# Split register loads, prompt masks from a table in DRAM, and a moved GpSimd addition in a four-layer fused kernel

## The reference

```python
def reference(x, ...):
    x = x + _L0_cond_ref(x, fside_Bx2_0, condB_angle)      # rotate/shift each image, bilinear gather
    x = x + _L1_cond_ref(x, itok_B_0_7, ...)               # FFN 512->2048->512, plus low rank parts by expert
    x = x + _L2_cond_ref(x, L2_cond_W1, L2_cond_b1, L2_cond_v, itok_B_0_2)
    x = x + _L3_cond_ref(x, itok_B_0_8, ...)               # adapter by language, then layer norm
    return x

def _L2_cond_ref(hidden, W1, b1, v, prompt_type_ids):
    scores = jnp.einsum('bsa,a->bs', jnp.tanh(jnp.einsum('bsd,da->bsa', hidden, W1) + b1), v)
    prefix_m, postfix_m, cloze_m = l <= j, l >= j, l != j
    mask = jnp.where(pt == 0, prefix_m[None], jnp.where(pt == 1, postfix_m[None], cloze_m[None]))
    p = jax.nn.softmax(jnp.where(mask, scores[:, None, :], NEG_INF), axis=-1)
    return jnp.einsum('bjl,bld->bjd', p, hidden) / cnt[..., None]

# end of _L3_cond_ref: x = hidden_states + adapted
    normed = (x - mean) * jax.lax.rsqrt(var + LN_EPS)
    return normed * gamma[language_ids][:, None, :] + beta[language_ids][:, None, :]
```

## Time and profile before

| | |
|---|---|
| median of 3 runs | 2572.32 us |
| profiled execution, own time | 2575.34 us |
| its span, first to last instruction | 2573.5 us |
| PE busy | 2274.3 us (88%) |
| DVE busy | 2052.4 us (80%) |
| POOL / ACT busy | 935.1 (36%) / 872.3 (34%) |
| mean granted TensorE clock | 0.928 of full |

### The profile page before, as it was taken

How to read it: one execution, slowest core, us unless ns; L and a number is a source line. 1 busy time by engine, 2 the same in 40 slices (tenths; PEclk the granted TensorE clock), 3 DMA queues, 4 the chain that set the end, 5 groups by cost and what they waited for, 6 DMA issues and landing times.

```text
span 2573.5 us, 53829 instructions
## 1 busy us (share of the span) xinstructions
PE 2274.3 (88%) x15550; PEld 1448.1 (56%) x15550; DVE 2052.4 (80%) x6404; ACT 872.3 (34%) x2292; POOL 935.1 (36%) x1317
## 2 busy tenths in 40 slices
PE   7998899888888888899888988889888989988896
PEld 5765555555655555455555555565555555555563
DVE  6346798888788888888888988888888888888853
ACT  1212333333333333333333333333333323333321
POOL 3213333444334434443344344433343444334201
PEclk6557999999999999999999999999999999999998
DMA  8553534455445434555454345454443445544311
GB/s 187 137 150 78 118 107 113 115 128 125 116 120 135 109 100 112 124 129 124 113 134 113 104 113 127 118 129 111 130 123 96 111 123 120 131 106 114 91 60 49
DMA packets 329295, 298.65 MB, mean 116 GB/s; under 512 B 190348, under 2 KB 250582, under 8 KB 328004
## 3 DMA queue, kind: packets, MB, share of 16 engines
q1 hardware_dynamic: 294116, 196.70, 31.3%
q0 software_dynamic: 33280, 92.31, 13.7%
q10 hardware_dynamic: 1632, 6.29, 0.8%
HBM read 269.54 MB, written 65.50 MB: 130 GB/s over the span
## 4 chain that ended last, share of the span: by engine, by line
DVE 51%; PE 29%; issue 11%; DVEq 7%; ACT 1%; POOL 1%; SPq 0%; DMA 0%; ACTq 0%; POOLq 0%
DVE work L832 13%; PE bank L1309 8%; PE bank L1332 7%; DVE y L932 5%; DVEq L817 5%; DVE work L845 4%; DVE work L846 4%; DVE work L844 4%; DVE work L855 3%; DVE hidden_parts L884 2%; DVEq L828 2%; DVE warp_sum L850 2%; DVE warp_sum L851 2%; PE bank L1217 2%; PE bank L1218 2%
## 5 line engine op out<-in xcount | busy, mean ns | idle before, releaser
L1332 PE MATMUL bank<-woT,hidden_parts 128*128 128x512 f16 x3072 | 782.0, 392 | 0.0
L1309 PE MATMUL bank<-x1T,wiT 128*128 128x256 f16 x6144 | 770.5, 276 | 9.2 <-ACT hidden_parts L1136 9.2
L832 DVE TENSOR_TENSOR work<-work 128x72 f32<-128x72 f32 x4096 | 724.0, 293 | 12.9 <-issue 7.4
L1309 PEld LDWEIGHTS bank<-x1T,wiT 128*128 128x128 f16 x6144 | 605.6, 99 | 153.5 <-issue 48.5
L568 POOL DMA_INDIRECT work<-strips,gather_now x512 | 564.0, 1101 | 158.9 <-issue 136.5
L1332 PEld LDWEIGHTS bank<-woT,hidden_parts 128*128 128x128 f16 x3072 | 264.2, 100 | 314.3 <-issue 33.9
L551 POOL TENSOR_TENSOR work<-group_now,frac_pix 128x256 f32<-128x256 f32 x256 | 157.3, 637 | 627.6 <-DVE work L846 626.5
L1134 ACT ACTIVATE hidden<-bank 128x256 f32<-128x256 f32 x512 | 195.3, 381 | 482.0 <-PE bank L1313 463.9
L564 POOL TENSOR_TENSOR gather_now<-group_now,no_offset 128x8 int32<-128x8 int32 x64 | 29.7, 463 | 627.1 <-DVE work L832 574.7
L884 DVE TENSOR_TENSOR hidden_parts<-hidden,hidden_parts 128x512 f16<-128x512 f32 x256 | 176.8, 691 | 54.1 <-ACT hidden_parts L1136 39.7
L1136 ACT ACTIVATE hidden_parts<-bank 128x256 f16<-128x256 f32 x512 | 194.8, 380 | 0.0
(11 more groups left out here) (191 smaller groups left out, 2585.7 us busy)
## 6 DMA issues: line engine op xcount, KB each, us to landing
strips<-in_x_dram SPq DMA_DIRECT2D x64, 532.0 KB
lw<-in_L_cond_W_dram SPq DMA_DIRECT2D x128, 256.0 KB
xs<-in_x_dram SPq DMA_DIRECT2D x64, 256.0 KB, 2.8
experts<-ib_dram SPq DMA_DIRECT2D x64, 256.0 KB
gamma_b<-in_L_cond_gamma_dram SPq DMA_DIRECT2D x64, 256.0 KB
beta_b<-in_L_cond_beta_dram SPq DMA_DIRECT2D x64, 256.0 KB
out_dram<-y SPq DMA_DIRECT2D x64, 256.0 KB, 2.1
work<-strips,gather_now POOLq DMA_INDIRECT x512
```

The costliest lines, as they stand in the source:

```text
L832: last = v.tensor_tensor(prods[:, :, :, j, :, row].rearrange("p a b g -> p g b a"), seen, wx.unsqueeze(2).broadcast_to([128, NG, TAPS, TAP ...
L1309: t.matmul(b[:, 0:2 * T], wiT[:, ws, m, tile(f)], x1T[:, xs_, m, :], start=(m == 0 and ws + xs_ == 0), stop=False)
L1332: last = t.matmul(down_ps[k][:, :], hidden_parts[:, hs, f % RING, k * T:(k + 1) * T], woT[:, ws, f, :], start=(first and n == 0), stop=False)
```

## The change

- The 32 registers of a half image are loaded in two loads of 16. The first stays in `sums` between L846 and L850. The second goes behind `hidden_low(1)` and `hidden_low(5)` for the second halves, and into `add_warp`, between the issue of the transpose and the wait for it, for the first halves of the next image.
- The three prompt masks are written to a table in DRAM once at the start. In each body SP reads the image's prompt number from `prompt_row` into a register and loads the mask by DMA into `masked`; DVE waits for `mask_in`. `begin_masks` is gone, and so is the instruction with `is_prefix` in `mask_scores`; a `memset` of the 128x1 column `neg_max` with a wait on it takes its place. The two subtractions that prepared the tables (L696) are gone.
- In POOL's body `deviations` comes before `add_beta`.

```diff
             sp.dma_start(expert_row[:, :], tok_expert.unsqueeze(0)).then_inc(in_loaded, 16)
+            sp.dma_start(prompt_row[:, :], tok_prompt.unsqueeze(0)).then_inc(in_loaded, 16)
             sp.wait_ge(set_ready, 1)
...
+            def load_mask(c, k):
+
+                prompt = sp.value_load(prompt_row[0:1, bass.ds(c * 2 + k, 1)], min_val=0, max_val=2)
+                ge(sp, probs_ready, c * 2 + (k - 1))
+                sp.dma_start(masked[:, k, :], mask_dram[bass.ds(prompt, 1)].squeeze(0)).then_inc(mask_in[k], 16)
+
             def store(c, k):
...
+            sp.wait_ge(consts_ready, 12)
+            sp.dma_start(mask_dram.rearrange("n p t -> p n t"), prompt_mask[:, :, :]).then_inc(mask_out, 16)
+            sp.wait_ge(mask_out, 16)
             sp.wait_ge(set_ready, 3)
...
                         load_expert_out(i, k)
+                for k in range(2):
+                    if there(i, 1):
+                        load_mask(i - 1, k)
                 for k in range(2):
...
                 if there(i, 2):
+                    deviations(i - 2)
                     add_beta(i - 2, q)
-                    deviations(i - 2)
                 if there(i, -1):
...
             link(v.reciprocal(inv_count[:, :], inv_count[:, :]))
-            for n in range(2):
-                link(v.tensor_tensor(prompt_mask[:, n, :], prompt_mask[:, n, :], prompt_mask[:, 2, :], ALU.subtract))
...
-                def load_offsets(h):
-
+                def load_offsets(h, part):
+
+                    n = LOADED // 2
+                    first = h * HALF + part * n
                     dve.wait_ge(dve_chain, offsets_here[0])
-                    v.load(regs, offs_now[0:1, h * HALF:(h + 1) * HALF])
+                    v.load(regs[part * n:(part + 1) * n], offs_now[0:1, first:first + n])
...
                     if then is not None:
-                        load_offsets(then)
+                        load_offsets(then, 0)
                     dve.wait_ge(taps_used, w * 4 + (k * 2 + h + 1))
...
-                def add_warp(k):
-
-                    link(v.transpose(warped.rearrange("p (w c j) -> p j w c", w=2, j=GP),
-                                     warp_sum[:, :].rearrange("p (j w c) -> p j w c", w=2, j=GP)))
+                def add_warp(k, then=None):
+
+                    count[0] += 1
+                    v.transpose(warped.rearrange("p (w c j) -> p j w c", w=2, j=GP),
+                                warp_sum[:, :].rearrange("p (j w c) -> p j w c", w=2, j=GP)).then_inc(dve_chain, 1)
+                    if then is not None:
+                        load_offsets(then, 1)
+                    dve.wait_ge(dve_chain, count[0])
                     dve.wait_ge(x_in[k], w * 16 + 16)
...
-                def begin_masks():
-
-                    ge(dve, probs_ready, c * 2)
-                    for k in range(2):
-                        last = v.scalar_tensor_tensor(masked[:, k, :], prompt_mask[:, 1, :], col(is_postfix, c * 2 + k),
-                                                      prompt_mask[:, 2, :], ALU.mult, ALU.add)
-                    link(last)
-
                 def mask_scores(k):
...
                     now = masked[:, k, :]
+                    dve.wait_ge(mask_in[k], c * 16 + 16)
                     dve.wait_ge(score_ps, n + 1)
-                    link(v.scalar_tensor_tensor(now, prompt_mask[:, 0, :], col(is_prefix, n), now, ALU.mult, ALU.add))
+                    link(v.memset(neg_max[:, k:k + 1], 0.0))
                     v.tensor_tensor_reduce(out=now, in0=mid_ps[:, 0:T], in1=now, scale=1.0, scalar=3e38,
...
                     take_offsets(0)
-                    load_offsets(0)
+                    load_offsets(0, 0)
+                    load_offsets(0, 1)
                     products(0, 0, 0, 16)
...
                     low_part(low_i, low_ps, low_i_hi, low_i_ready)
-                if tail:
-                    begin_masks()
-
                 def products_between(k, h, g):
...
                 hidden_low(1)
+                if warp:
+                    load_offsets(1, 1)
                 if there(i, 2):
...
                     sums(0, 1, 0)
-                    add_warp(0)
+                    add_warp(0, 0)
                 hidden_low(3)
...
                 hidden_low(5)
+                if warp:
+                    load_offsets(1, 1)
                 products_between(1, 1, 6)
...
                     sums(1, 1, 0 if ahead else None)
-                    add_warp(1)
+                    add_warp(1, 0 if ahead else None)
                 hidden_low(7)
```

More of the change, by code:

```diff
@@ L115, in build @@
         expert_row = sb("expert_row", [1, B], i32)
+        prompt_row = sb("prompt_row", [1, B], i32)
         N_WIN, N_PROD, N_TAPS = 2 * NG * RUN, TAPS * TAPS * D // 2, 2 * TAPS * D
@@ L211, in build @@
         lang_in = [sem("lang_in0"), sem("lang_in1")]
+        mask_out = sem("mask_out")
+        mask_in = [sem("mask_in0"), sem("mask_in1")]
         stored = [sem("stored0"), sem("stored1")]
@@ L270, in there @@
             return not isinstance(i, int) or first <= i < NP + first
-        def col(table, n):
-            return table[:, bass.ds(n, 1)]
         room = woT[:, :, :, :].rearrange("p s t d -> p (s t d)").bitcast(fp32)
@@ L654, in _ @@
             v.memset(ang[:, B:B + 1], 0.0).then_inc(set_ready, 1)
-            dve.wait_ge(in_loaded, 16 * 7)
+            dve.wait_ge(in_loaded, 16 * 8)
             dve.wait_ge(consts_ready, 12)
```

1 line of the change is left out of this document (added).

## The result

The changed kernel takes 2657.8 us (median of four runs, 2623.5 to 2670.6) against 2570.9 for the kernel before on the same chip: 1.029 of it, 95% interval 1.019 to 1.039. It is slower by 2.9%; the forecast was 4.5% faster. The profiled execution took 2656.0, its span 2654.1, at a mean granted TensorE clock of 0.932.

A forecast was written before the change was run, and what follows sets the result against it. DVE and PE taking turns bound the kernel. 70 us (x3, x1), 36 and 31 (boundaries), 3 at the start less 2 at the end, made 138; less 23 for half clock, 115: 2457 us, range 2430 to 2508.

The forecast's parts named there:

- 1.36 in the forecast: DVE's way to x3 in each full body: 0.15 + 0.81 from split loads and 0.4 from masks.
- Rival 4: x3 no earlier for PE, ACT sitting in `hat` behind POOL's L551 and gather: up to 1.36 x 30 lost, 2498; chance 0.06.
- Rival 3: Slower: the load of 16 registers hardly shorter than that of 32; at 1.85 us a load, 2625 us; chance 0.03.
- one-victim rule: DVE instructions with two SBUF inputs and GpSimd instructions reading SBUF exclude each other; moving beta exchanges victims; fully blocked products cost 2.48.
- The split loads: Register loads in `sums`: 16 take 1.15 us, each wait 0.95 shorter, added loads costing 0.8 or 0.14; 0.96 before x3 and x1.
- The masks: `begin_masks` counted nothing, `mask_scores` 0.2 twice before x3; the mask's DMA lands by 1174, before its read after 1176.25.
- L932 at 0.75: DVE's multiplication by gamma at a body's end, no longer beside POOL's beta: 0.75 instead of 3.90, 3.15 us less.
- Full clock behind x1: PE's stretch L1166 to L1370 takes 7.15 instead of 9.95: 2.80 gained at L1370, against 1.22 if the clock falls.
- What beta costs elsewhere: Beta (L595) beside next body's residuals and six products costs 1.3, bounds 0 and 2.48; L1313 1.85 earlier at straight boundaries.
- Rival 1: The stall moves with beta: half clock stays at x1, products lose all 2.48; put at 2482 us, chance 0.30.
- 0.77 for the clock: Deduction of 23 us over the span: some 15 PE stretches staying or newly at half clock, 1.58 each.
- The chance of 0.04 for slower: Covers a load of 16 hardly shorter than 32 (0.03) and masks landing late (0.02); faster had 0.94.

The follow-up runs named there:

- e7_gap1: The changed kernel with DVE waiting once for its own product, behind the sixth product of image 1's first half; 2486.5 us, 0.967 of the kernel before.
- e6_masks_beta: The changed kernel without the split register loads, so masks by DMA and POOL's new order only; 2576.2 us, 1.001 of the kernel before.
- e1_split: The kernel before with the split register loads alone; 2706.5 us, 1.043 of the kernel before.
- e12_before_gap: The kernel before with one wait of DVE behind the sixth product of image 1's first half, nothing else; 2581.6 us, 1.003 of the kernel before.
- e2_masks: The kernel before with the masks by DMA alone; 2568.2 us, 0.996 of the kernel before.
- e3_beta: The kernel before with POOL's Newton steps ahead of the addition of beta, nothing else; 2563.5 us, 0.994 of the kernel before.
- e5_delay: The kernel before with POOL's gather of image 0 put off by three repeats of a small addition; 2803.0 us, 1.091 of the kernel before.
- e11_delay_gap: The kernel before with gather of image 0 put off by three repeated additions and one DVE wait behind the sixth product; 2658.4 us, 1.032 of the kernel before.
- e8_one_input: The changed kernel with the 32 products of image 1's first half replaced by copies with one SBUF input; 2522.3 us in one run.

## Why the prediction was wrong, point by point

The table sets stages of a body beside each other, mean of 24 bodies of the loop, from start to start; from L1370's start the two kinds of boundary are apart (behind a branch / straight). The 3.95 us from x1 of image 0 to x3 of image 1 are the same everywhere and left out.

| stage | before | after | e7_gap1 | e6_masks_beta |
|---|---|---|---|---|
| first `hidden_low` to x1 of image 0 | 21.34 | 20.15 | 20.16 | 20.88 |
| x3 to x1 of image 1 | 28.58 | 33.90 | 28.39 | 28.44 |
| x1 of image 1 to L1370 | 10.43 | 8.13 | 7.96 | 9.26 |
| L1370 to the next first `hidden_low` | 11.08 / 7.20 | 10.89 / 8.70 | 10.98 / 8.60 | 12.42 / 9.37 |
| whole body | 73.44 | 75.93 | 70.25 | 73.42 |

**The step that failed** is one that isn't in the sum. Each edit was costed on DVE's and PE's path, and POOL's gather was taken as it stood, as if its DMAs took 0.95 wherever they fall. The 1.2 us that x3 gained (1.36 in the forecast) moved DVE's products over the eighth DMA: 5.3 us more in the second stage on average, which is 7.0 in the bodies with a held DMA and nothing in the others. 24 eighth DMAs were held, some 168 us, against 171 between after and e7_gap1. No rival had it. Rival 4 named the engines and the place (ACT sits in `hat` behind POOL's L551 and gather, so x3 helps PE nothing), but its price was only the loss of the gain, 1.36 a body, because it had POOL late by nothing of its own; it should have asked what POOL runs beside after the shift. Rival 3, the one that ended slower, was the wrong mechanism: the load does scale.

The Trainium skill had half of the warning, in the section that the prediction cites for its one-victim rule (SBUF — State Buffer, Who interferes with whom): a DMA stalled by a DVE instruction is one whose descriptors GpSimd generates, and it is GpSimd that is starved of the port. But for the very instruction at stake, a `tensor_tensor`, the same section says that it was not seen to stall a DMA, and infers a reason. Here the traces decide, and they say otherwise: products, which are `tensor_tensor`, held it for up to 6.04 us, over some 25 of them and the `hidden_low` between them. I had used the section for the multiplication by gamma and for beta and had not asked what it means for L568, either way.

**The split loads: right in mechanism, too large by a term that was missing.** Loads of 16 (view of single lines: count, ns shortest/median/longest):

```profile
L831 DVEq TENSOR_LOAD <-offs_now x256: 1095/1099/1350, 108.9 to 2531.4; - x128
```

1.10 where I took 1.15 (from 263 ns for one register, which is the shortest of the earlier trace rows; the median, 285, gives 1.16). DVE's own wait ahead of each sum is 1.0 shorter (forecast 0.95), and the loads behind `hidden_low` cost 0.7 and 0.9 (counted 0.8 each). The way to x3 is 0.74 shorter in e1_split, where I had 0.96, and 1.17 in after with the masks (forecast 1.36). The way to x1 is 0.19 shorter in e7_gap1 with its pause, which alone cost 0.20 there in e12_before_gap, so about 0.4 where I took 0.96. The trace of after shows the missing term:

```profile
755.61 1.39 POOL L565 TENSOR_TENSOR work<-group_now,frac_pix 128x256 f32<-128x256 f32 x2 [7.49 <-DVE work L860]
755.82 0.70 DVE L864 TENSOR_TENSOR warp_sum<-work 128x256 f32<-128x256 f32 x1 [0.29 <-DVE work L860]
```

POOL's `add_fractions` is released by DVE's L860 (L846 of before). In before it ran in the 1.28 us in which DVE sat waiting for its registers, and cost nobody anything. With that wait gone, DVE's two additions stand beside it in the first half of each image and take 0.70 and 0.73 instead of 0.42 each: nearly 0.6 lost before x3 and again before x1 (means of e7_gap1). The wait that the change removed had been the cover of another engine's work.

**The masks: as forecast.** DVE does not wait for them, and the way to x3 is 0.44 shorter in e2_masks (forecast 0.4). In time they gave 9 us alone and 22 on top of the split loads, where the terms gave 0.4 x 30 = 12.

**L932 at 0.75: right.** Single lines of after (L943 is L932 of before, 909 median in the earlier trace rows):

```profile
L943 DVE SCALAR_TENSOR_TENSOR y<-y,mv,gamma_b x64: 750/752/1079, 351.0 to 2641.1; 128x512 f32<-128x512 f32 x64
```

**Full clock behind x1: right** in after and e7_gap1: x1 to L1370 is 2.30 and 2.47 shorter, forecast 2.80. One such stretch of after, behind a wait for x1 of 1.80 (busy time by stretch, the columns of the earlier trace rows, where it was 0.50):

```profile
1192.20:1195.60 3.40, 3.40 (x23) 1.62 (x24) 3.25 (x5) 0.60 (x1) 2.77 (x4) 1.00 0.49 139
```

Without the split (e6_masks_beta) the wait for x1 stays, the clock falls (0.51 in the stretch read above), and it is 1.17, close to the 1.22 counted for that case.

**What beta costs elsewhere: right where DVE is early, wrong where it is late.** The forecast had beta beside two residuals and six products, 1.3 lost. In e7_gap1 a straight boundary shows just that (timeline):

```profile
1120.76 2.51 POOL L609 TENSOR_TENSOR x<-x,beta_b 128x512 f32<-128x512 f32 x2
...
1121.87 2.17 DVE L846 TENSOR_TENSOR work<-work 128x72 f32<-128x72 f32 x6
...
1124.70 0.28 PE L1328 MATMUL bank<-low_i,experts 128*128 128x256 f16 x1 [2.05 <-DVE low_i L894]
```

Six products take 2.17 instead of 1.06, and PE waits 2.05 for `low_i` where 1.9 was forecast. From L1370 on, e7_gap1 gives back 1.40 straight and nothing behind a branch (forecast 0.95 and nothing). Rival 1, full blocking of products, is what e3_beta and e6_masks_beta do (2.1 a body).

**The sum without the hold.** 1.36 + 0.96 + 2.80 - 0.48 a body less 0.77 for the clock was 3.87; e7_gap1 shows 73.44 - 70.25 = 3.19, or 3.47 without its pause. Over the span it gained 86, with the 8 of the pause 94, where I had 115. So the forecast of 2457 would have been some 20 us too low even if no DMA had been held; 2508, the upper end, would have covered it. The chance of 0.04 for slower was the grave error: the sum rested on terms for two engines, while a third engine's DMAs lay 0.2 to 0.3 us from the products.

## What to carry to other kernels

When an edit shifts one engine by a microsecond, list what the other engines run in the shifted window, GpSimd's indirect DMAs above all, and look at the longest duration of their line: 4679 against a median of 947 ns was in before's trace already. If they fall into a long unbroken stretch of DVE, one wait of DVE for its own instruction behind their start costs 0.28 us and can save 7. Before you remove an idle wait, see which engine worked undisturbed in it: here 0.6 of the 1.0 us gained in each image's first half went back that way. And measure parts together as well as alone: masks and beta gave 9 and 14 us alone, nothing together, and 55 on top of the split loads. Look then at the idle time behind the branch before you credit an edit with 10 us.

## What the runs showed of the hardware

- An indirect DMA that POOL begins well inside an unbroken run of DVE's products (`tensor_tensor` on SBUF data) is not slowed but held: every held one ends 0.78 to 0.79 us behind the last product, in before, after, e1_split, e5_delay and e11_delay_gap alike, 103 of them in runs of 16 or more. In ten traces, where at least 1 us of the run was left, all 150 DMAs begun from 0.4 us ahead of the first product to 0.48 behind it took 0.94 to 1.04; of 54 begun 0.51 to 0.63 behind it 21 were held; of 87 begun 0.84 or more behind it 82 were, and the five exceptions stand near 250 us, in the early bodies.
- A pause of 0.15 us in the run is enough to let the DMA go (1.33 instead of up to 6.0). Behind the pause it counts as a new run: begun 0.62 us behind it the DMA took 0.95, begun 0.94 behind it 4.66.
- The holder loses nothing: 16 products take 2.64 us with the held DMA beside them, as in the earlier trace rows without POOL.
- Copies with one SBUF input hold it otherwise (e8_one_input): two DMAs to 0.79 us behind the last copy, twelve to 0.12 behind the last of sixteen, and eleven were let go in the midst of the copies.
- Against plain POOL instructions it is the products that lose: 3.54 instead of 1.39 us for eight beside beta, and 0.70 and 0.73 instead of 0.42 for DVE's two additions beside `add_fractions`.
- Behind the loop's branch DVE sits idle with nothing in the profile waited for, 0.36 to 4.50 us on average depending on the kernel; no row says what sets it.
- A load of registers from SBUF takes 285, 1099 and 2102 ns (medians; the first 263 at least) for 1, 16 and 32 of them, the first on SP and the others on DVE.
